# Maxima over one half of the keys first, and the second half's first stacks moved to the head of attention

## What is computed

```python
q = (src @ q_w).reshape(b, s, h, hd).transpose(0, 2, 1, 3)
k = (src @ k_w).reshape(b, s, h, hd).transpose(0, 2, 1, 3)
v = (src @ v_w).reshape(b, s, h, hd).transpose(0, 2, 1, 3)
scores = jnp.einsum('bhqd,bhkd->bhqk', q, k) / np.float32(np.sqrt(hd))
scale = jax.nn.sigmoid(jnp.einsum('bhsd,hd->bhs', q, scale_w)) * 2.0
scores = scores * scale[..., None]
aw = jax.nn.softmax(scores, axis=-1)
out = jnp.einsum('bhqk,bhkd->bhqd', aw, v)
```

## Time and profile before

| | us |
|---|---|
| median of three runs | 2605.64 |
| lowest and highest of them | 2603.2, 2606.28 |
| profiled execution | 2591.33 |
| its span, first to last instruction | 2589.5 |
| TensorE matmul busy | 2426.2 |
| VectorE busy | 2118.5 |
| ScalarE busy | 1768.4 |
| GpSimd busy | 994.4 |

### The profile page before, as it was taken

One profiled execution on the slowest core, in us unless ns is written; L12 is line 12 of the kernel. 1 busy time (PEld: TensorE's weight loads), 2 busy tenths in 40 slices (PEclk: granted clock), 3 DMA queues, 4 the chain that ended last, 5 costly groups with the idle time before them and its releaser, 6 DMA issues. The chain is left out here.

```text
span 2589.5 us, 45166 instructions
## 1 busy us (share of the span) xinstructions
PE 2426.2 (94%) x16296; PEld 1078.1 (42%) x16296; DVE 2118.5 (82%) x4221; ACT 1768.4 (68%) x2303; POOL 994.4 (38%) x1188
## 2 busy tenths in 40 slices
PE   6799999999858999999999999999999999786996
PEld 6366666666533223222222222222232332574554
DVE  4577867888768999999899899898999993593887
ACT  2677787777522777878777787787787788212664
POOL 1377877888851122221221221212210111344564
PEclk9899999999988999999999999999999999876998
DMA  2322232322240040404003030040030000215883
GB/s 91 95 81 78 90 100 80 99 93 88 72 141 18 14 62 13 63 14 63 13 14 50 14 57 7 14 63 14 11 52 2 1 2 1 94 61 192 281 283 110
DMA packets 111810, 174.13 MB, mean 67 GB/s; under 512 B 19290, under 2 KB 86514, under 8 KB 106452
## 3 DMA queue, kind: packets, MB, share of 16 engines
q1 hardware_dynamic: 103684, 155.20, 22.5%
q0 software_dynamic: 6016, 14.49, 1.5%
q10 hardware_dynamic: 1888, 1.56, 0.2%
HBM read 145.28 MB, written 27.02 MB: 67 GB/s over the span
## 5 line engine op out<-in xcount | busy, mean ns | idle before, releaser
L1588 DVE TENSOR_REDUCE max_part<-round_psum 128x1 f32<-128x512 f32 x2048 | 1269.3, 683 | 101.8 <-PE round_psum L1502 96.9
L1554 ACT ACTIVATE p_exp<-score_psum 128x1024 f32<-128x1024 f32 x1024 | 993.4, 1022 | 216.2 <-PE score_psum L1489 210.7
L1502 PE MATMUL round_psum<-k_stack,q_stack 64*128 64x512 bf16 x2048 | 705.9, 385 | 19.9 <-DVE pv_psum L1580 8.5
L1480 PE MATMUL score_psum<-q_stack,k_stack 64*128 64x512 bf16 x2048 | 599.7, 379 | 0.9 <-ACT p_exp L1554 0.2
L1489 PE MATMUL score_psum<-q_stack,k_stack 35*128 35x512 bf16 x2048 | 595.2, 378 | 0.4 <-DMA q_stack<-max_rows 0.4
L1530 PE MATMUL pv_psum<-p_exp,values 128*17 128x512 f32 x4096 | 539.6, 598 | 0.0
L1502 PEld LDWEIGHTS round_psum<-k_stack,q_stack 64*128 64x128 bf16 x2048 | 189.4, 93 | 609.3 <-DVE max_part L1588 512.1
L628 PE MATMUL rot<-tokens_t,w_in 128*128 128x512 f32 x576 | 271.5, 603 | 16.6 <-DVE bc_conv L780 13.4
L1489 PEld LDWEIGHTS score_psum<-q_stack,k_stack 35*128 35x128 bf16 x2048 | 188.9, 94 | 116.8 <-DMA q_stack<-max_rows 0.9
L1622 POOL TENSOR_TENSOR rden<-pv_out,minus_one 128x16 f32<-128x16 f32 x32 | 92.9, 2902 | 359.1 <-ACT pv_out L1572 356.8
L1480 PEld LDWEIGHTS score_psum<-q_stack,k_stack 64*128 64x128 bf16 x2048 | 139.4, 94 | 59.7 <-ACT p_exp L1554 26.4
(11 more groups left out here) (265 smaller groups left out, 3553.4 us busy)
## 6 DMA issues: line engine op xcount, KB each, us to landing
expert_w<-in_expert_w SPq DMA_DIRECT2D x39, 1028.0 KB, 6.6
cum_rows_in<-cum_rows SPq DMA_DIRECT2D x64, 512.0 KB, 3.8
cum_pairs_in<-cum_rows SPq DMA_DIRECT2D x120, 128.0 KB, 3.8
qk_rows<-qk_parts SPq DMA_DIRECT2D x64, 192.0 KB, 3.1
q_stack<-qk_rows SPq DMA_DIRECT2D x84, 128.0 KB, 7.8
k_stack<-qk_rows SPq DMA_DIRECT2D x84, 128.0 KB, 8.8
token_rows<-tokens SPq DMA_DIRECT2D x12, 512.0 KB, 3.1
x_in<-in_x SPq DMA_DIRECT2D x8, 512.0 KB, 8.5
```

The source lines that it names most:

```text
L1480: nc.tensor.matmul(ebank[i // 2][:, i % 2, :], ks[rows, n % 2, plane, k * P:(k + 1) * P], qs[rows, n % 2, plane, q * BLK:(q + 1) * BLK], s ...
L1502: nc.tensor.matmul(bank[step][:, :], qs[rows, n % 2, plane, at:at + P], ks[rows, n % 2, plane, keys * BLK:(keys + 1) * BLK], start=True, s ...
L1554: nc.scalar.activation(pt[:, (k * 2 + pair) % 4, :, :], ebank[pair][:, :, :], ACT.Exp).then_inc(*exped.up(u, k, pair))
L1588: nc.vector.tensor_reduce(mx[:, c * HG + h, keys:keys + 1], bank[step][:, :], AX_X, ALU.max).then_inc(*maxed.up(u, k, i))
```

## The change

Four things. The list of SyncE in stage 3 loses "stack1". `attention_order` begins with six "stack" entries for group 0, half 1. Group 0's first half gets a semaphore of its own, `first_stacked`; the one that TensorE waited for before now counts the second half alone, and TensorE waits for the first half at the very first maximum and for the second at step 8 of unit 0 (for later groups at step 0, as before). And `max_at` orders the maxima of every unit by the half of the keys: its first eight steps take blocks of keys 0 and 1 for all heads and queries, its last eight take 2 and 3.

```diff
+        self.first_stacked = sems.dma("stack_first", [(0, 0, t, kind, odd) for t in range(TERMS) for kind in "qk"
+                                                      for odd in range(2)])
         self.stacked = [sems.dma(f"stack{slot}", [(n, j, t, kind, odd) for n in range(slot, len(GROUPS), 2)
-                                                         for j in stack_halves(n) for t in range(TERMS)
+                                                         for j in stack_halves(n)[-1:] for t in range(TERMS)
                                                          for kind in "qk" for odd in range(2)]) for slot in range(2)]
...
+    stacked = S.first_stacked if (n, j) == (0, 0) else S.stacked[slot]
...
-                              rows[odd]).then_inc(*S.stacked[slot].up(n, j, t, kind, odd))
+                              rows[odd]).then_inc(*stacked.up(n, j, t, kind, odd))
...
-    "SP": "weights0 load4 weights1 fill load7 load5 keep4 load6 save0 keep5 stack0 save1 stack1 keep6 keep7",
+    "SP": "weights0 load4 weights1 fill load7 load5 keep4 load6 save0 keep5 stack0 save1 keep6 keep7",
...
-    p, rest = divmod(k, 2 * CPB)
-    return 2 * p + i % 2, rest // 2, 2 * (rest % 2) + i // 2
+    half, rest = divmod(k, KT // 2)
+    p, c = divmod(rest, CPB)
+    return 2 * p + i % 2, c, 2 * half + i // 2
...
+    for t in range(TERMS):
+        yield "stack", 0, 1, t
     for t in range(-LEAD, total + 4):
...
-                    if q == 0 and k == 0 and i == 0:
+                    if (u, k, i) == (0, 0, 0):
+                        pe.wait_ge(*S.first_stacked.all())
+                    if q == 0 and k == (0 if n else KT // 2) and i == 0:
                         pe.wait_ge(*S.stacked[n % 2].at(n, 1, TERMS - 1, "k", 1))
```

## The result

| | before | after |
|---|---|---|
| median, us | 2602.81 | 2592.78 |
| lowest and highest | 2597.24, 2606.51 | 2590.87, 2595.28 |
| profiled execution, its span | 2591.33, 2589.5 | 2591.18, 2589.4 |

By the medians the changed kernel is faster by 10.0 us. The ratio, taken by itself, is 0.9968 with a 95% interval of 0.9955 to 0.9981, which is a gain of 8.3 us, between 4.9 and 11.7. Measured a second time it was 0.9957 (0.9938 to 0.9975), 11.2 us, between 6.5 and 16.1. The forecast was a gain of 5.6 us, which the first interval still holds and the second doesn't, and a time of 2600.0, with a range down to 2596.0. And the two profiled executions are equally long. A gain above the forecast, and two traces that show none of it, need an explanation, and they have one in common.

A forecast was written before the change was run, and what follows sets the result against it. SyncE's stack1 issues were taken to hold the border ahead of attention, whose maxima keep VectorE busy. Removing them gains 5.6 us, all other terms zero: 2605.64 - 5.6 = 2600.0 us, range 2596.0 to 2604.3.

The forecast's parts named there:

- What ends last at the border: Stage 3 to attention: SP's list ends last, ACT next; without stack1 the first maximum comes 5.6 us earlier.
- The price of the issues in attention, and the new wait: Attention's head: twenty-four issues on SP delay no one; stacks land 7 to 13 us before step 8; cost zero.
- Order of the maxima, transfers beside them: In attention: new order zero, within 0.2 us; transfers beside maxima no cost, bound 0.1 us on each of four steps.
- The bare tail of stage 3: End of stage 3, formerly hidden by SP: a later full clock would show about 2.2 us, in the new kernel alone.
- The clock at the head: Attention's start: TensorE still begins at the lower clock for as long as before; zero shift, 1.4 us either way.
- the second rival: Attention's head: clock stays up or rises sooner after the shorter pause; gain 7 to 9.7 us, chance 0.18.
- the clock also fell behind 830.5 without a pause: In attention, from 830.6 us the clock was low (0.50) without such a pause; argued against the sooner-clock rival, chance 0.18.
- The reading of one trace: Attention's head in the profiled execution: full clock only 11.4 us after the first maximum, taken to last as long after the change.
- The 14.3 us between the profiled execution and the median: Whole kernel: timed median 2605.64 lay 14.3 us above the profiled execution's 2591.33; unexplained and carried over unchanged.

The follow-up runs named there:

- the variant with the thin stretch filled: Changed kernel plus sixteen bfloat16 matmuls, one behind each maximum between the last values step and the first scores; ratio to before 0.9965.
- the filled kernel of before: Kernel before plus eight matmuls with unread results in TensorE's pause at the end of stage 3; ratio to before 0.9979, 5.5 us faster.

## Why the prediction was wrong, and where it was right

- **What ends last at the border:** right. SP's list was the last by 5.7 us, ACT was next, and the first maximum follows its drain at 0.95 us. SP was through 6.8 us ahead of ACT, where the prediction had 8: its two last issues took 1.71 us and not 0.97. With ACT last this costs nothing.
- **The price of the issues in attention, and the new wait:** right. In the trace nothing waits for these transfers, and the second half is in 16 us ahead of step 8; I had said 7 to 13, with fewer slow steps.
- **Order of the maxima, transfers beside them:** right, zero. 1360.1 us from first to last weighing after, 1360.0 before.
- **The bare tail of stage 3:** a cost in the new kernel alone, which I allowed for, isn't seen. ACT's drain stands 53.2, 53.3 and 55.8 us behind the scan stage's last matmul before, and 53.7, 55.6, 54.4 and 53.2 after: the same spread, and no shift that these traces show. What I had wrong is that SP hid this spread before. In the trace of before with 55.8, SP's drain too stands 2.7 us later behind the scan stage, 61.5 us against 58.8 in the other two. And the spread goes with the clock in this stage: in each trace it fell 31 to 34 us behind the scan stage's last matmul; in those where it stayed low for some 14 us the drain stands at 53.2 to 53.7, in those where it stayed low for some 17 at 54.4 to 55.8. No run tests which of the two makes the other. This is how the first maximum of the second measurement came to lie 3.3 us earlier within its stage and not 5 to 6.
- **The clock at the head:** this step failed. I wrote that "the head still starts at the lower level and needs as long as before", hence zero, and that the clock terms "are a spread and not a shift". In the changed kernel the clock fell just about at the first maximum and three times in four came back after 3.5 us (and once more in the variant with the thin stretch filled, whose head is the same); before, it had been low for 5 us when the first maximum came and stayed so for 11.4 to 18.5 more. The term was 0 and measured 3.9 us. What I had named as the second rival (the clock comes up sooner, because the pause is short) with a chance of 0.18 is what mostly happens, and even that was sized small: it had three slow steps to win back, a head of 11.4 us, where the usual head of before has about 18. The reason that I gave against it, that the clock also fell behind 830.5 without a pause, was no evidence on how long it stays low.
- **The reading of one trace:** I took 11.4 us for what a head of before costs, and it was the shortest of the three seen. The rule that I cited from the Trainium skill (TensorE: Matmul & The Clock Gate, section "What's actually happening"), that the number of slow matmuls differs between runs of one kernel, holds here: 3.5 and 16.7 us in traces of the same kernel. It should have kept me from using one trace as the mean. That both kernels would draw from the same spread doesn't follow from it; that was my addition, and it is what was wrong.
- **The 14.3 us between the profiled execution and the median,** for which I had no reason and which I carried over, is explained in part. The profiled one had 171 us of low clock where the average is 187, and 16 us at 0.35 is 5.5. The median itself came out 2.8 us lower with more executions. The other 6 us have no row. This is why the time was missed by more than the gain: 2600.0 - 2592.78 = 7.2 us, of which 2.8 are a level taken too high and 4.4 a gain taken too small. With the later median the range would have begun at 2593.2.

Not settled: why the clock stays low for 3.5 us in some executions after a pause of 2.9 us and for 16.7 in another. Four traces of the changed kernel and three of before give the 3.9 us with a standard error of some 1.6 us, an estimate from their scatter. That the head's clock is worth some microseconds doesn't hang on it: the filled kernel of before won 5.5 us with its border untouched. Border and head together, 5.7 + 3.9 = 9.6 us, lie within the intervals of both measurements, 8.3 and 11.2 us.

## What to carry to other kernels

When a wait at a border between stages is removed, price two things: the silence itself, and what TensorE's idle time does to the clock of the work behind it; here the second was worth about two thirds of the first (3.9 against 5.7 us). A pause of TensorE ahead of a stage that it bounds can be shortened or filled with a few matmuls whose result nobody reads. In the stretch that VectorE bounds, such matmuls were worth nothing. And before a term is taken from one trace, look whether the profiled execution is a typical one: its time against the median and its mean granted clock tell.

## What the runs showed of the hardware that I had not expected

- How long the clock was low at the head went with the length of TensorE's pause ahead of it, though not evenly. After pauses of 1.1 to 1.7 us (three kernels) the head had no time at the lower level; after 2.5 to 2.9 us (six traces) 3.5 us in four of them and 14.1 and 16.7 in two; after 8.3 to 8.6 us (four traces) 11.4 to 18.5 us, and after 15.1 us (one trace) 18.5, no more than that. Most of the kernels have one trace only.
- A microsecond at the lower level goes with 0.35 us on average over the whole kernel, and with about 0.4 at attention's head (64.6 - 59.3 = 5.3 us for 13.2). In the stretch where VectorE is busy for 15.0 of 15.3 us, 3.2 us less of it brought no gain.
- The scan stage, with identical code, ended anywhere from 718.4 to 728.1 us. What makes it vary wasn't looked into.
